# Two-layer graph attention on one core: the LayerNorm normalisations moved from VectorE to ScalarE

## What is computed

```python
# layer 0, one head; the mask comes from the adjacency
scores = (q @ k.T) / sqrt(256);  scores = where(adj == 0, -1e18, scores)
attn = where(adj == 0, 0, softmax(scores))
x0 = x + (attn @ x) @ Wc
xn = (x0 - mean(x0)) * rsqrt(var(x0) + 1e-5) * gamma + beta
# layer 1, eight heads of 32 channels
logits = q @ k.T / sqrt(32) + log(clip(adj, 1e-8))
z = xn + (softmax(logits) @ v) @ Wo.T + bo
out = (z - mean(z)) * rsqrt(var(z) + 1e-5) * gamma + beta
```

## Time and profile before

| what | us |
|---|---|
| median of 3 runs | 1387.14 |
| lowest and highest | 1383.5, 1393.78 |
| the profiled execution, its own time | 1384.42 |
| its span in the trace | 1382.3 |
| TensorE busy | 1258.6 (91%) |
| VectorE busy | 961.7 (70%) |
| GpSimd busy | 740.3 (54%) |
| ScalarE busy | 518.6 (38%) |
| mean granted clock of TensorE | 0.958 |

### The profile page before, as it was taken

How to read it: one execution, slowest core, us unless ns; L and a number is a source line. 1 busy time by engine, 2 the same in 40 slices (tenths; PEclk the granted TensorE clock), 3 DMA queues, 4 the chain that set the end, 5 groups by cost and what they waited for, 6 DMA issues and landing times.

```text
span 1382.3 us, 21749 instructions
## 1 busy us (share of the span) xinstructions
PE 1258.6 (91%) x6758; PEld 725.6 (52%) x6758; DVE 961.7 (70%) x1736; ACT 518.6 (38%) x940; POOL 740.3 (54%) x359
## 2 busy tenths in 40 slices
PE   6789999999999999999999999998999999899873
PEld 4564554646555464655546455554645555464411
DVE  4474867868576786857678685767858576785863
ACT  2133523444343344434333443433434243343330
POOL 0035456474636647463664746366473646747473
PEclk9789999999999999999999999999999999999876
DMA  3050311405032140513214050321405132130300
GB/s 115 0 138 16 111 49 50 113 15 137 31 94 61 51 114 15 137 31 90 62 53 114 15 137 31 90 62 56 111 15 135 32 84 68 55 112 15 91 16 15
DMA packets 69651, 94.66 MB, mean 68 GB/s; under 512 B 14081, under 2 KB 32769, under 8 KB 69634
## 3 DMA queue, kind: packets, MB, share of 16 engines
q1 hardware_dynamic: 69634, 94.44, 24.8%
HBM read 35.40 MB, written 8.39 MB: 32 GB/s over the span
## 4 chain that ended last, share of the span: by engine, by line
issue 31%; PE 26%; POOL 23%; DVE 12%; ACT 5%; POOLq 1%; DMA 1%; DVEq 0%; SPq 0%; ACTq 0%
POOL PR L1037 19%; PE misc L525 5%; PE misc L601 5%; PE values L665 4%; PE scores L644 4%; DVE mx L897 3%; DVE sums_w L944 3%; PE denominators L665 3%; POOL z L1049 3%; ACT PR L760 1%; DVE CLIP L871 1%; POOL rstd L1028 1%; PE misc L623 1%; DVE K1L L862 1%; ACT K1H L738 1%
## 5 line engine op out<-in xcount | busy, mean ns | idle before, releaser
L1037 POOL TENSOR_TENSOR PR<-PR,CLIP 128x1024 f32<-128x1024 f32 x224 | 551.2, 2477 | 514.6 <-ACT PR L760 514.4
L897 DVE TENSOR_REDUCE mx<-misc 128x1 f32<-128x512 f32 x512 | 323.7, 681 | 163.4 <-PE misc L623 161.2
L760 ACT ACTIVATE PR<-scores 128x512 f32<-128x512 f32 x512 | 277.8, 597 | 282.0 <-PE scores L644 281.9
L644 PE MATMUL scores<-QS,KS 97*128 97x512 f32 x512 | 193.1, 459 | 3.6 <-DMA QS<-nm 1.9
L665 PE MATMUL values<-PR,V 128*32 128x512 f32 x1024 | 141.1, 624 | 46.2 <-ACT sums_v L770 28.8
L623 PE MATMUL misc<-K1H,Q1H 32*128 32x512 f32 x512 | 133.0, 503 | 16.5 <-DVE K1L L862 10.2
L665 PE MATMUL denominators<-PR,ones 128*32 128x512 f32 x1024 | 145.9, 644 | 0.0
L644 PEld LDWEIGHTS scores<-QS,KS 97*128 97x128 f32 x512 | 90.8, 196 | 95.5 <-issue 48.6
L601 PE MATMUL misc<-U,P 128*128 128x257 f32 x512 | 128.4, 394 | 0.0
L623 PEld LDWEIGHTS misc<-K1H,Q1H 32*128 32x128 f32 x512 | 53.7, 184 | 141.0 <-issue 47.5
L944 DVE RECIPROCAL sums_w<-sums_w 128x128 f32<-128x128 f32 x128 | 111.8, 915 | 9.1 <-ACT sums_v L770 9.1
(11 more groups left out here) (148 smaller groups left out, 2013.4 us busy)
## 6 DMA issues: line engine op xcount, KB each, us to landing
ADJ<-adj_t SPq DMA_DIRECT2D x16, 1024.0 KB, 6.0
QS<-Q1H SPq DMA_DIRECT2D x256, 64.0 KB, 2.0
KS<-K1H SPq DMA_DIRECT2D x256, 64.0 KB, 2.0
P<-x_t SPq DMA_DIRECT2D x16, 512.0 KB, 3.7
X<-x SPq DMA_DIRECT2D x16, 512.0 KB, 3.7
QS<-Q1L SPq DMA_DIRECT2D x128, 64.0 KB, 2.0
KS<-K1L SPq DMA_DIRECT2D x128, 64.0 KB, 2.0
out<-z SPq DMA_DIRECT2D x16, 512.0 KB, 3.0
```

The lines of the kernel that those rows point to most:

```text
L644: pe.matmul(ST[n][:], KS[:, h, P * k:P * (k + 1)], QS[:, h, :], start=True, stop=True).then_inc(scores_filled, 1)
L760: act.activation(PR[quad % WEIGHT_BUFFERS][:, h, :], ST[n][:], ACT.Exp, scale=SCALE1).then_inc(exp_done, 1)
L897: dve.tensor_reduce(mx1[:, g, h, t:t + 1], misc_bank(ph, "max1", g, n)[:], AX.X, ALU.max, negate=True).then_inc(misc_drained["dve"], 1)
L1037: pool.tensor_tensor(w, w, clipped, ALU.mult).then_inc(masked_pool, 1)
```

## The change

Both normalisations are computed on ScalarE as rstd * x + centre, where centre = -mean * rstd for each node. VectorE computes centre in one instruction of 128x4 per normalisation (four tiles, one value per partition and tile) once GpSimd has the reciprocal root. ScalarE runs four Identity activations of 128x256, with a scale and a bias of one value per partition, where the list has norm0 and norm1. The list itself stays as it is. The wait for the residual (res_ready) goes with norm0 to ScalarE. TensorE, GpSimd and SyncE have no change; they wait on the same semaphores (xn_ready, zn_ready) as before.

```diff
@@ buffers and semaphores
+        centre0 = sb("centre0", [P, T])
+        centre1 = sb("centre1", [P, T])
+        centre0_ready = sem("centre0_ready")
+        centre1_ready = sem("centre1_ready")
@@ block.scalar
+            def norm0(ph):
+                act.wait_ge(centre0_ready, ph.j + 1)
+                if ph.back:
+
+                    act.wait_ge(res_ready, ph.i + 1)
+                for t in range(T):
+                    act.activation(xn[:, t, :], X[:, t, :], ACT.Identity, bias=centre0[:, t:t + 1],
+                                   scale=rstd0[:, t:t + 1]).then_inc(xn_ready, 1)
+
+            def norm1(ph):
+                act.wait_ge(centre1_ready, ph.t + 1)
+                for t in range(T):
+                    act.activation(z[:, t, :], z[:, t, :], ACT.Identity, bias=centre1[:, t:t + 1],
+                                   scale=rstd1[:, t:t + 1]).then_inc(zn_ready, 1)
+
             do = {
-                "prepare": prepare, "split": split,
+                "prepare": prepare, "split": split, "norm0": norm0, "norm1": norm1,
@@ block.vector
             def norm0(ph):
                 dve.wait_ge(rstd0_ready, ph.j + 1)
-                if ph.back:
-
-                    dve.wait_ge(res_ready, ph.i + 1)
-                for t in range(T):
-                    dve.tensor_scalar(xn[:, t, :], X[:, t, :], mv0[:, t, 0:1], rstd0[:, t:t + 1],
-                                      ALU.subtract, ALU.mult).then_inc(xn_ready, 1)
+                dve.scalar_tensor_tensor(out=centre0[:], in0=mv0[:, :, 0], scalar=-1.0, in1=rstd0[:],
+                                         op0=ALU.mult, op1=ALU.mult).then_inc(centre0_ready, 1)
@@
             def norm1(ph):
                 dve.wait_ge(rstd1_ready, ph.t + 1)
-                for t in range(T):
-                    dve.tensor_scalar(z[:, t, :], z[:, t, :], mv1[:, t, 0:1], rstd1[:, t:t + 1],
-                                      ALU.subtract, ALU.mult).then_inc(zn_ready, 1)
+                dve.scalar_tensor_tensor(out=centre1[:], in0=mv1[:, :, 0], scalar=-1.0, in1=rstd1[:],
+                                         op0=ALU.mult, op1=ALU.mult).then_inc(centre1_ready, 1)
```

## The result

The changed kernel takes 1422.63 us (median of 4 runs, 1419.71 to 1426.44) against 1386.82 for the kernel before (4 runs, 1383.5 to 1393.78). The ratio is 1.0255, with a 95% interval from 1.0227 to 1.0282: slower by 2.6%. The prediction was 1422 us. The profiled execution took 1424.58 us, with a span of 1422.8; the span before was 1382.3.

A forecast was written before the change was run, and what follows sets the result against it. The prediction took the hand-over from exp(2,1) on ScalarE through GpSimd to the values matmuls as the bound. 26.6 + 7.5 + 1 + 0.8 + 0.8 = 36.7 us on 1384.42 gave 1421.1, stated as 1422 us, range 1406 to 1440.

The forecast's parts named there:

- The bound and norm1: Steady phases: norm1's activations delay exp(2,1), GpSimd's masks and quad 3's values matmuls, +1.9 us each, +26.6 us over 14.
- The hold: Four norm1 activations ahead of exp(2,1) on ScalarE: 0.475 us a step, 1.9 us in all (1.45 to 2.25).
- norm0: Before exp(5,1): mask(5,1) comes late at quad 5's values matmuls, +0.2 us in ten phases, +1.1 in five, 7.5 us.
- The step that failed: After quad 5's values matmuls: TensorE's existing wait for K1L absorbs delay, 0.40 us in phases that already waited for GpSimd.
- The clock rival: TensorE's new stand at scores(3,0) lowers its clock: 0.95 us a phase, 13 us more, 1435 us; chance 0.18.
- Ends: Last phase with scores: VectorE's slow norm1 goes, but exp(2,1) and mask(2,1) are held instead, +1 us (-0.9 to +1.9).
- the small instruction: VectorE's 128x4 instruction replacing four per normalisation, taken as 0.17 us.
- the first norm0: First normalisation at the kernel's start, bare with nothing to cover it: +0.8 us.
- the final phase: Bare chain at the kernel's end: small instruction 0.2 us and four activations 2.0 in place of 1.38, +0.8 us.
- The last step to 1422: From the summed 1421.1 us to 1422, given a median 2.7 us above the profiled execution.
- The relief of VectorE: VectorE's removed normalising work was costed at 0; the faster rival had it win 22.3 us, 1362 us, chance 0.06.
- The absorbed shift: Rival: something unseen in the GpSimd stretch takes up exp(2,1)'s delay, leaving 7 to 10 us, 1393 us; chance 0.11.

The follow-up runs named there:

- the late norm0: Changed kernel with norm1 moved behind denominators1 0 and norm0 behind exp(5,1) in ScalarE's list: 1391.52 us, ratio 1.0042 to the kernel before.
- the double hold: Changed kernel with four more activations of the same form ahead of norm1's, into a spare buffer nobody reads: 1469.44 us.
- VectorE with its full load: Changed kernel with VectorE still running its eight normalising instructions a phase, into a spare buffer nobody reads: 1427.0 us.
- the early place: Changed kernel with norm1 moved behind denominators1 0 in ScalarE's list, where ScalarE stands idle, not ahead of exp(2,1): 1390.27 us.

## Why the prediction was right, point by point

**The bound and norm1.** The chain through exp(2,1), GpSimd and the values matmuls was the right one, and the shares of busy time the wrong guide. The hold was put at 1.9 us (0.475 a step) and measured 1.97 (0.49 a step, 588 ns each); the assumed 0.09 us for the scale was measured as 0.09. Of the 1.97, C shows 1.83. The 0.02 us a step that the prediction adds for a source in SBUF has no row beside it there; in the kernel before, casts of 128x512 take 621 ns from SBUF (XTH<-P) and 602 from PSUM (XNH<-misc), which bears it out. The rule for the duration in the Trainium skill (ScalarE: Activation LUTs, What ACT_TABLE_LOAD costs), an estimate of 1.97 us, agrees with the trace. Over 14 phases that is 25.6 us, predicted 26.6.

**norm0: the size was about right, the path only half.** The prediction said that mask(5,1) comes late at the values matmuls of quad 5, with +1.1 us in phases where these waited already and +0.2 in the others. Measured are +0.94 us in phases that were at the full clock and nothing in the others; over the 15 stretches A this sums to 5.7 us, predicted 7.5. The two kinds of phase are the same two, but what divides them is the granted clock: at the lower clock TensorE is late itself and covers the delay (in the phase of the earlier trace rows, XNH started 5.41 us behind the start of A already before). The late mask did come, with 1.46 us at its start for the 1.5 predicted and 0.94 at the values matmuls. The step that failed is the one behind it, that K1L stays where it was and gives TensorE 0.4 us back. K1L is itself 0.93 us later, since XNH stands behind the four activations, and with the mask back at its time this alone keeps the price, as the late norm0 shows. That 1.1 and 0.94 lie close together is in part luck. I had written that xn comes 0.8 us later but in time for the transposes, and didn't ask what else stands in ScalarE's queue between norm0 and XNH.

**The clock rival came in part.** It was given 0.18, as a thing that happens in every phase or in none, at 0.95 us a phase. It happens in five phases, with 0.86 us each, 4.3 us. With the double hold it happens in all of them.

**Ends.** The last phase with scores was put at +1. From its sums to the values matmuls of quad 3 it takes 63.25 us, against 60.93: +2.3. VectorE, ScalarE and GpSimd there, in the changed kernel:

```profile
1351.85 1.43 DVE L992 SCALAR_TENSOR_TENSOR centre<-mv,rstd 128x4 f32<-128x4 f32 x1
...
1353.31 2.07 ACT L798 ACTIVATE z<-z,centre,rstd 128x256 f32<-128x256 f32 x4 [4.36 <-DVE centre L992]
...
1356.42 2.36 POOL L1051 TENSOR_TENSOR PR<-PR,CLIP 128x1024 f32<-128x1024 f32 x1 [3.17 <-ACT PR L764]
1358.74 2.36 POOL L1063 TENSOR_TENSOR z<-z,spread 128x1024 f32<-128x1024 f32 x1
```

GpSimd's output starts 53.79 us behind the start of A, before 51.49 (1319.63 behind 1268.14), and this is the whole +2.3. The mis-sized term is the small instruction, which ran beside a mask and took 1.43 us in place of the 0.17 predicted; ScalarE stood idle and waited for it. That is 1.3 of the 2.3 (1.43 less 0.17, an estimate). TensorE's own stand of 3.44 us there is not the cause, since the values matmuls of quad 3 still waited 2.61 us for GpSimd. The kernel is 0.6 us late where the first A starts, as the first norm0 was predicted to cost 0.8, and the final phase takes 0.8 more from the reciprocal root on, as predicted.

**The sum** of these is 25.6 + 5.7 + 4.3 + 2.3 + 0.6 + 0.8 = 39.3, of 40.5 us between the spans. The rest is 0.6 us in the stretches B and 0.6 between those values matmuls and the last reciprocal root. The predicted sum was 36.7: a little too much for norm1 and norm0, and too little for the clock and the last phase. These errors in part cancel. The last step to 1422 is also loose: the prediction's own 1421.1 and 2.7 make 1423.8.

**The relief of VectorE** was costed at nothing and is worth nothing: VectorE with its full load gives the same stretches. The prediction read GpSimd as idle beside norm1; it was in a mask until 758.61 (5.08 us before 763.69), and there the small instruction took 0.44 us. **The absorbed shift** fell with the 7.03 us of GpSimd's idle time.

## What to carry to other kernels

An engine that is 38% busy is not free: what counts is which instruction stands next in its queue where the work is put in, and how soon somebody waits for that one. Here the same four instructions cost 2 us a phase ahead of an exponential that feeds the slowest chain, and nothing some instructions earlier, where the engine was idle. When a total moves by a few us, cut the phases at the same waits and compare stretches, since a clock that drops in more or fewer phases can hide or double the effect of an edit in the total.

## What the runs showed of the hardware that was not expected

A VectorE instruction on 128x4 took 2.20 us. It is the small product for centre1 at the early place. It started at 757.71, in a GpSimd mask that ran from 757.51 to 759.89, and ended at 759.91. In the changed kernel it started at 777.51, when a mask (775.55 to 777.93) was near its end, took 0.44 us and ended with it. The same form beside an idle GpSimd takes 0.16; the instructions of both lines in the changed kernel (ns, min, median, max):

```profile
L951 DVE SCALAR_TENSOR_TENSOR centre<-mv,rstd x16: 161/163/164, 58.0 to 1305.8; 128x4 f32<-128x4 f32 x16
L992 DVE SCALAR_TENSOR_TENSOR centre<-mv,rstd x16: 163/440/1430, 190.7 to 1412.4; 128x4 f32<-128x4 f32 x16
```

The prediction took 0.17 us for both. For centre1 it was 0.44 us in the steady phases, which cost nothing because ScalarE asked for it some four microseconds later, and 1.43 us in the last phase with scores, where ScalarE waited for it. The maxima on VectorE (L916) run beside masks at their usual 0.68 us. The Trainium skill (GPSIMD Engine Reference, Specifications) says that GpSimd's SBUF interfaces are shared with VectorE, with contention for VectorE instructions that have two SBUF inputs; the trace agrees, and adds that such an instruction ended only with the whole mask, however small it was.

The second surprise is the clock. The same stand of 1.91 us is followed by the lower level in 9 of 14 phases of the kernel before and in none of the 14 with norm1 alone moved, and a stand of 1.23 us in 5 of the 14 steady phases of the changed kernel. So the length of the stand alone doesn't decide it. What does was not tried and stays open; so does the 0.11 us in C.
